# Toeplitz operands of 64 rows instead of 128, read from eight shifted copies of each head's taps

## The chip, the cores and the metric

One Trainium2 chip, one of its cores. The metric is the device time of one execution in microseconds (us), as a median over runs. Lower is better.

## What is computed

The input x is (64 batches, 32 heads, 512 positions), float32. The first layer is a causal convolution along the positions: each head has a filter of 512 taps, made from 64 complex modes, and the result is kept only where the position is below the batch's length. Added to x, it goes through a gated linear layer with low-rank (LoRA) additions chosen per batch. The case is about the first layer.

```python
def _get_kernel(log_dt, C, log_A_real, A_imag, length):     # K: the taps, heads x 512
    ...
    K = 2.0 * jnp.einsum('hn,hnl->hl', Cs, jnp.exp(P)).real
...
y = jnp.fft.irfft(u_f * k_f, n=n)[..., :Lq]                 # causal convolution of u with K
y = y + u_m * D[:, None]
return y * mask[:, None, :]
...
x = x + _L0_cond_ref(x, ...)        # convolution layer
x = x + _L1_cond_ref(x, ...)        # gate, up, silu, down, each with a low-rank part
```

## The kernel before

**Stages.** From 0 to about 20 us the taps of head group 0 are prepared; from there to about 79 us the convolution of 16 pairs of heads runs, with the taps of groups 1 to 3 prepared in between; from 80 us to the end the second layer runs, 16 tiles of 128 rows, with TensorE almost always busy.

**Taps.** The 32 heads are four groups `g` of eight. For each, VectorE makes phases (`phases(g)`), ScalarE sines (`trig(g)`), VectorE tables (`tables(g)`), TensorE multiplies them (`taps(g)` in the tensor block, L1025), and VectorE copies the result to `k_sb` (`taps(g)` in the vector block, L786 and L787), which raises `k_ready`. `store_taps(g)` writes the 16 KB to the DRAM tensor `kpad` (L255), a row for each head: 128 zeros and then 512 taps. A pair of heads is `pair`, so that group `g` holds the pairs 4g to 4g+3.

**Convolution.** A Toeplitz matrix is a window that slides over the taps: partition p of it is the row of taps shifted by p. `load_toep` (L261) builds it with one DMA from `kpad`: 128 partitions x 2 heads x 512 elements, each partition starting one element later, 512 KB for a pair. `load_um` (L266) loads the pair's input (256 KB), with its 128 positions of a block in reverse order. `conv(pair)` (L1038) makes eight float32 matmuls, four for each head: 128 rows are contracted, 128 columns of weights are `toep`, and 256, 192, 128 and 64 columns of `um` stream through. A float32 matmul appears in the trace as two weight loads and two matmuls, so a pair is 16 of each. Both heads' results share one PSUM bank of 512 columns. `add_conv(pair)` (L814) on VectorE selects the result into `x` with one COPY_PREDICATED of 128x512.

**Rings.** `toep`, `um` and the PSUM banks `ps_c` each have RC = 4 slots: `load_um` and `load_toep` wait on `conv_ps` until the pair four before is done, and `conv` waits on `x1_ok` until the pair four before has been added.

**Order.** All transfers are issued by SyncE (SP) in one written order, and a wait in it holds back everything behind it. After group 0 is stored come one weight piece (L244, 352 KB), the four `toep` of pairs 0 to 3, three more pieces, half of x for group 1 (512 KB), and so on; from pair 8 on a loop issues `um` and `toep` pair by pair, with the first LoRA tables among them (`a_raw`, four of 152 KB, behind pair 8; `b_raw`, four of 64 KB, behind pair 9), and behind it the six pieces of `wd`. On VectorE the order is `phases(1)`, `phases(2)`, `tables(1)`, `phases(3)`, `taps(1)`, the copy of `amask_t`, `add_conv(0)`, `tables(2)`, `tables(3)`, `taps(2)`, `add_conv(1)`, `taps(3)`, and then the pairs. On TensorE it is taps 0, pair 0, taps 1, pairs 1 and 2, taps 2, pair 3, taps 3, and then pairs 4 to 15. GpSimd makes the low parts of eight weight pieces (L439) once all taps are ready. ScalarE makes their high parts.

## Time and profile before

| | |
|---|---|
| median of 3 runs | 532.95 us (532.25 to 535.38) |
| the profiled execution: its time | 533.11 us |
| the profiled execution: span of the core | 531.4 us |
| the profiled execution: mean granted TensorE clock | 0.997 |
| TensorE matmul busy | 494.7 us (93%) |
| VectorE / ScalarE / GpSimd busy | 292.3 / 198.0 / 46.4 us |
| DMA traffic | 82.74 MB, mean 156 GB/s |

The span in 40 slices of 13.3 us each. A digit is the busy share of a slice in tenths, PEclk the granted clock in tenths of full speed, DMA the mean busy share of the 16 DMA engines. The convolution stage is in slices 3 to 6: there DMA stands at 9, and TensorE has slices below 9.

```profile
## 2 busy tenths in 40 slices
PE   0098799999999999999999999999999999999997
PEld 0087787989898999999999999898989898989986
DVE  7883176846454555546464547373737474545541
PEclk9999899999999999999999999999999999999999
DMA  7899995556555656555555656464646465555520
GB/s 288 267 346 376 331 340 128 122 111 154 116 152 115 144 128 147 126 137 118 142 123 138 130 129 139 108 157 109 157 88 174 101 161 114 153 117 148 110 63 21
```

A timeline row is start, duration, engine, line, operation, output<-input, shapes, count. PE is TensorE's matmul, PEld its weight load, SPq the queue of SyncE.

### The profile page before, as it was taken

The page shows a single profiled execution, that of the slowest core. Times are in us where ns is not written, and L with a number is a line of the kernel's source. Part 1 is how long each engine was busy: PE and PEld are TensorE (multiplying, and loading weights), DVE is VectorE, ACT ScalarE, POOL GpSimd, SP SyncE. Part 2 cuts the span into 40 slices and gives each one's busy share as a digit, 9 for nine tenths or more (in the row PEclk, how much of TensorE's full clock was granted, in tenths as well). Part 3 has the DMA queues.
Part 4 walks back from the last instruction along what each step waited for, and adds up shares of the span by engine and source line. Part 5 has one row for each costly group of instructions (what it writes and reads, how often), then busy time and mean ns, then how long its engine had stood idle before and what let it go on. Part 6 is the DMA issues. An engine that isn't in the chain of part 4 may idle for free.

```text
span 531.4 us, 9990 instructions
## 1 busy us (share of the span) xinstructions
PE 494.7 (93%) x2940; PEld 449.0 (84%) x2940; DVE 292.3 (55%) x617; ACT 198.0 (37%) x411; POOL 46.4 (9%) x55
## 2 busy tenths in 40 slices
PE   0098799999999999999999999999999999999997
PEld 0087787989898999999999999898989898989986
DVE  7883176846454555546464547373737474545541
ACT  5791006433333334334342333243434243434330
POOL 1006600100000001000000101010101010101000
PEclk9999899999999999999999999999999999999999
DMA  7899995556555656555555656464646465555520
GB/s 288 267 346 376 331 340 128 122 111 154 116 152 115 144 128 147 126 137 118 142 123 138 130 129 139 108 157 109 157 88 174 101 161 114 153 117 148 110 63 21
DMA packets 175443, 82.74 MB, mean 156 GB/s; under 512 B 128034, under 2 KB 157282, under 8 KB 175426
## 3 DMA queue, kind: packets, MB, share of 16 engines
q1 hardware_dynamic: 175426, 82.54, 60.5%
q8 instruction: 8, 0.13, 0.1%
q14 instruction: 9, 0.07, 0.0%
HBM read 63.46 MB, written 19.04 MB: 155 GB/s over the span
## 4 chain that ended last, share of the span: by engine, by line
PE 88%; DMA 5%; DVE 5%; issue 1%; SPq 0%; ACT 0%; DVEq 0%
PE ps_g L1111 23%; PE ps_u L1111 22%; PE ps_db L1072 13%; PE ps_da L1072 13%; PE ps_x L1064 3%; PE ps_g L1038 3%; DMA toep<-kpad 2%; DMA kpad<-k_sb 2%; PE ps_g L1121 2%; PE ps_u L1122 2%; PE ps_g L1122 2%; PE ps_u L1121 2%; PE ps_u L1038 2%; PE ps_da L1178 1%; PE ps_db L1179 1%
## 5 line engine op out<-in xcount | busy, mean ns | idle before, releaser
L1111 PE MATMUL ps_g<-w_hi,x_hi 128*128 128x512 f32 (+1 forms) x192 | 72.7, 379 | 1.4 <-DVE x_lo L995 1.4
L529 ACT CAST b_spl<-b_raw 64x512 fp32r<-64x512 f32 (+1 forms) x96 | 51.7, 571 | 55.3 <-PE ps_u L1122 35.7
L1111 PE MATMUL ps_u<-w_lo,x_hi 128*128 128x512 f32 (+1 forms) x192 | 71.4, 372 | 0.0
L1111 PE MATMUL ps_u<-w_hi,x_lo 128*128 128x512 f32 (+1 forms) x192 | 71.4, 372 | 0.0
L1111 PE MATMUL ps_g<-w_hi,x_lo 128*128 128x512 f32 (+1 forms) x192 | 71.4, 372 | 0.0
L1111 PE MATMUL ps_u<-w_hi,x_hi 128*128 128x512 f32 (+1 forms) x192 | 71.4, 372 | 0.0
L1111 PE MATMUL ps_g<-w_lo,x_hi 128*128 128x512 f32 (+1 forms) x192 | 70.9, 369 | 0.0
L876 DVE TENSOR_TENSOR b_spl<-b_raw,b_spl 64x512 fp32r<-64x512 f32 (+1 forms) x96 | 57.9, 629 | 15.3 <-ACT b_spl L529 13.7
L933 DVE TENSOR_TENSOR h_act<-h_act,ps_u 128x512 f32<-128x512 f32 (+1 forms) x48 | 30.4, 632 | 58.6 <-PE ps_u L1122 38.9
L1072 PE MATMUL ps_da<-wd_hi,ht_hi 128*128 128x288 f32 (+1 forms) x176 | 52.1, 296 | 0.0
L1072 PE MATMUL ps_da<-wd_lo,ht_hi 128*128 128x288 f32 (+1 forms) x176 | 51.9, 295 | 0.0
L1072 PE MATMUL ps_db<-wd_lo,ht_hi 128*128 128x288 f32 (+1 forms) x176 | 51.9, 295 | 0.0
L1072 PE MATMUL ps_db<-wd_hi,ht_hi 128*128 128x288 f32 (+1 forms) x176 | 51.9, 295 | 0.0
L1072 PE MATMUL ps_db<-wd_hi,ht_lo 128*128 128x288 f32 (+1 forms) x176 | 51.9, 295 | 0.0
L1072 PE MATMUL ps_da<-wd_hi,ht_lo 128*128 128x288 f32 (+1 forms) x176 | 51.8, 294 | 0.0
L464 POOL COPY xt<-x 128x512 f32 (+1 forms) x15 | 13.7, 911 | 397.1 <-DMA a_raw<-atab 397.1
L543 ACT CAST ht_hi<-h_raw 128x512 fp32r<-128x512 f32 (+1 forms) x45 | 24.7, 548 | 49.4 <-DMA h_raw<-hrow 49.4
L1111 PEld LDWEIGHTS ps_g<-w_hi,x_hi 128*128 128x128 f32 x192 | 36.1, 188 | 5.8 <-issue 1.5
L1111 PEld LDWEIGHTS ps_u<-w_hi,x_lo 128*128 128x128 f32 x192 | 36.1, 188 | 5.8
L1111 PEld LDWEIGHTS ps_u<-w_hi,x_hi 128*128 128x128 f32 x192 | 36.1, 188 | 5.8
L1111 PEld LDWEIGHTS ps_u<-w_lo,x_hi 128*128 128x128 f32 x192 | 36.1, 188 | 5.8
L1111 PEld LDWEIGHTS ps_g<-w_hi,x_lo 128*128 128x128 f32 x192 | 36.0, 188 | 5.7
(170 smaller groups left out, 887.7 us busy)
## 6 DMA issues: line engine op xcount, KB each, us to landing
a_raw<-atab SPq DMA_DIRECT2D x64, 152.0 KB, 2.3
toep<-kpad SPq DMA_DIRECT2D x16, 512.0 KB, 7.3
b_raw<-btab SPq DMA_DIRECT2D x128, 64.0 KB, 2.1
h_raw<-hrow SPq DMA_DIRECT2D x30, 256.0 KB, 2.9
um<-xr SPq DMA_DIRECT2D x16, 256.0 KB, 5.4
x<-xT SPq DMA_DIRECT2D x8, 512.0 KB, 6.9
w_raw<-wgu SPq DMA_DIRECT2D x8, 512.0 KB, 9.1
xrow<-x_sq SPq DMA_DIRECT2D x64, 64.0 KB, 2.2
```

The costliest lines, as they stand in the source:

```text
L464: nc.gpsimd.tensor_copy(xt[:, :, :].rearrange("p k (h b) -> p k h b", b=BT), x[:, :, :, bass.ds(t * BT, BT)].rearrange("p h k b -> p k h b ...
L529: nc.scalar.copy(b_spl[b_rows(slot), up, 0:w], b_raw[b_rows(slot), up * w:(up + 1) * w]).then_inc(b_hi, 1)
L543: nc.scalar.copy(ht_hi[:, f0:f0 + full, :], raw[:, 0:full, :]).then_inc(hthi_ok, 1)
L876: V.tensor_tensor(b_spl[b_rows(1 - slot), up, 0:w], b_raw[b_rows(slot), up * w:(up + 1) * w], b_spl[b_rows(slot), up, 0:w].bitcast(F32), A ...
L933: V.tensor_tensor(h_act[:, 0:w], h_act[:, 0:w], ps_u[s][:, 0:w], ALU.mult).then_inc(act_ok, 1)
L1038: last = T.matmul(ps_c[slot][:, at + d * NB:at + KB * NB], toep[:, slot, h, d * P:(d + 1) * P], v, start=(d == 0), stop=(d == KB - 1))
L1064: ins = T.matmul(ps_x[0][:, 0:P], w, xt[:, kb, :], start=(kb == 0), stop=(kb == KB - 1))
L1072: ins = T.matmul(ps[:, 0:c1 - c0], hs[0:rows, f, :], ws[0:rows, f, c0:c1], start=(f == 0 and hs is ht_hi and ws is wd_hi), stop=(bank == 1 ...
L1111: T.matmul(ps[:, 0:w], xs[:, kb, :], ws[:, kb, col:col + w], start=(kb == 0 and xs is x_hi and ws is w_hi), stop=False)
L1121: T.matmul(ps[:, 0:w], t_hi[:, up, :], b_spl[:, up, 0:w], start=False, stop=False)
L1122: T.matmul(ps[:, 0:w], t_lo[:, up, :], b_spl[:, up, 0:w], start=False, stop=True).then_inc(u_ps if up else g_ps, 1)
L1178: T.matmul(ps_da[:, 0:DA_W], ts[:, :], bd_spl[:, 0:DA_W], start=False, stop=end)
```

## The change

Both heads of a pair are handled side by side in 64 rows each. A Toeplitz operand for a head has now 64 partitions of HW = 576 elements; head 0 of the pair lies in partitions 0 to 63, head 1 in 64 to 127. A block of 128 positions is contracted in two halves of 64, so a head needs eight matmuls of 64 rows instead of four of 128. The matmuls alternate between the two heads, and each head writes a PSUM bank of its own (columns 0 to 255 of it). The rings become six slots for `toep` and `um` (RT, RU) and three double banks for the results (RP), one of them `ps_x`.

For group 0 each head's operand is loaded straight from `kpad`, two DMAs for a pair. For groups 1 to 3 a new DRAM tensor `krep` holds, for each head, eight copies of the taps, each shifted by eight elements (NCP = 8, ROWS = 8); `copy_taps(g)` writes them from `kpad` with one DRAM-to-DRAM DMA for the group, and `load_toep` reads both heads over 128 partitions with one DMA. The order of transfers is written anew, and on VectorE `taps(1)` moves ahead of `phases(3)`.

```diff
+RT = 6
+RU = 6
+RP = 3
+HR = P // 2
+HW = NL + HR
+NCP = 8
+ROWS = HR // NCP
+CW = HW + ROWS
...
+        krep = nc.dram_tensor("krep", (NH * NCP, CW), F32, kind="Internal")
...
-            toep = sb(pa, "toep", [P, RC, 2, NL])
-            um = sb(pa, "um", [P, RC, 2 * KB * NB])
+            toep = sb(pa, "toep", [P, RT, HW])
+            um = sb(pa, "um", [P, RU, 2 * KB * NB])
...
+        ps_c = [top.enter_context(nc.psum_tensor(name, [P, 2, 512], F32)) for name in ("ps_gg", "ps_uu", "ps_xx")]
+        ps_g, ps_u, ps_x = ([both[:, i, :] for i in range(2)] for both in ps_c)
...
-            return bass.AP(tensor=kpad, offset=pair * (2 * (P + NL)) + 1, ap=[[1, P], [P + NL, 2], [1, NL]])
+        def direct_taps(pair, h):
+
+            return bass.AP(tensor=kpad, offset=(2 * pair + h) * (P + NL) + 1, ap=[[1, HR], [1, HW]])
+
+        def copied_taps(pair):
+
+            return bass.AP(tensor=krep, offset=2 * pair * NCP * CW, ap=[[CW, 2 * NCP], [1, ROWS], [1, HW]])
...
+            def copy_taps(g):
+
+                sp.wait_ge(k_out[g], 16)
+                from_ = bass.AP(tensor=kpad, offset=g * HG * (P + NL) + 1, ap=[[P + NL, HG], [ROWS, NCP], [1, CW - 1]])
+                into = bass.AP(tensor=krep, offset=g * HG * NCP * CW, ap=[[NCP * CW, HG], [CW, NCP], [1, CW - 1]])
+                sp.dma_start(into, from_).then_inc(k_rep[g], 16)
+
+            def load_toep(pair):
+
+                slot, g = pair % RT, pair // RC
+                if g == 0:
+                    sp.wait_ge(k_out[0], 16)
+                    for h in range(2):
+                        sp.dma_start(toep[h * HR:(h + 1) * HR, slot, :], direct_taps(pair, h)).then_inc(toep_in[slot], 16)
+                else:
+                    sp.wait_ge(k_rep[g], 16)
+                    wait(sp, conv_ps, pair - RT + 1)
+                    sp.dma_start(toep[:, slot, :], copied_taps(pair)).then_inc(toep_in[slot], 16)
...
             store_taps(0)
+            for pair in range(RC):
+                load_toep(pair)
             load_piece(2 * KB)
-            for pair in range(RC):
-                load_toep(pair, pair, 0)
-            for n in range(2 * KB + 1, NP_GU):
-                load_piece(n)
+            load_piece(2 * KB + 1)
             load_x(1, 0)
+            for pair in range(RC, RU):
+                load_um(pair)
             store_taps(1)
             load_x(1, 1)
             load_x(2, 0)
...
+            copy_taps(1)
+            for pair in range(RU, 2 * RC - 1):
+                load_um(pair)
+            load_toep(RC)
+            load_um(2 * RC - 1)
+            load_toep(RC + 1)
+            load_toep(RC + 2)
+            load_x(2, 1)
+            store_taps(2)
+            load_toep(RC + 3)
+            load_um(2 * RC)
+            copy_taps(2)
+            store_taps(3)
+            load_x(3, 0)
+            copy_taps(3)
+            load_toep(2 * RC)
+            load_um(2 * RC + 1)
+            load_toep(2 * RC + 1)
+            load_piece(2 * KB + 2)
+            load_x(3, 1)
+            load_piece(2 * KB + 3)
...
+            taps(1)
             phases(3)
-            taps(1)
...
             def conv(pair):
-                slot = pair % RC
-                pe.wait_ge(toep_in[slot], 16 * (pair // RC) + 16)
-                pe.wait_ge(um_in[slot], 16 * (pair // RC) + 16)
-                wait(pe, x1_ok, pair - RC + 1)
-                for h in range(2):
-                    at = h * KB * NB
-                    for d in range(KB):
-                        v = um[:, slot, h * KB * NB:h * KB * NB + (KB - d) * NB]
-                        last = T.matmul(ps_c[slot][:, at + d * NB:at + KB * NB], toep[:, slot, h, d * P:(d + 1) * P],
-                                        v, start=(d == 0), stop=(d == KB - 1))
+                slot = pair % RT
+                pe.wait_ge(toep_in[slot], toep_need(pair))
+                pe.wait_ge(um_in[pair % RU], 16 * (pair // RU) + 16)
+                wait(pe, x1_ok, pair - RP + 1)
+                if pair == RP - 1:
+                    pe.wait_ge(amaskt_ok, 1)
+                for d in range(KB):
+                    for half in range(2):
+                        at = d * P + (1 - half) * HR
+                        for h in range(2):
+                            rows = slice(h * HR, (h + 1) * HR)
+                            v = um[rows, pair % RU, half * KB * NB:half * KB * NB + (KB - d) * NB]
+                            last = T.matmul(ps_c[pair % RP][:, h, d * NB:KB * NB], toep[rows, slot, at:at + P], v,
+                                            start=(d == 0 and half == 0), stop=(d == KB - 1 and half == 1))
                 last.then_inc(conv_ps, 1)
```

## Rows read from the trace of the kernel before

**Rows 1.** Chain of work that ended last, 15 to 82 us: start, us, what.
```profile
22.15 5.37 DMA toep<-kpad
27.56 4.95 PE ps_g L1038 x16
39.85 9.13 DMA kpad<-k_sb
...
79.03 0.20 DVE x L822
```

**Rows 2.** Timeline of TensorE: pairs 0 to 4, taps, and later pairs.
```profile
27.56 4.95 PE L1038 MATMUL ps_g<-um,toep 128*128 128x256 f32 x16 [7.55 <-DMA toep<-kpad]
32.44 0.96 PE L1025 MATMUL ps_db<-e 128*32 128x16 f32 x16
42.78 2.62 PE L1038 MATMUL ps_g<-um,toep 128*128 128x256 f32 x16 [0.66 <-DMA toep<-kpad]
46.82 2.62 PE L1038 MATMUL ps_g<-um,toep 128*128 128x256 f32 x16 [1.42 <-DMA toep<-kpad]
...
60.26 4.29 PE L1038 MATMUL ps_g<-um,toep 128*128 128x256 f32 x16 [2.08 <-DMA toep<-kpad]
64.39 4.98 PE L1038 MATMUL ps_u<-um,toep 128*128 128x256 f32 x32
69.20 4.98 PE L1038 MATMUL ps_g<-um,toep 128*128 128x256 f32 x32
74.01 4.98 PE L1038 MATMUL ps_u<-um,toep 128*128 128x256 f32 x32
```

**Rows 3.** Busy time by stretch: us, busy (x) by engine, PEclk, DMA share, GB/s.
```profile
42.78:64.38 21.60, 17.00 (x96) 15.57 (x97) 4.78 (x7) 1.14 (x2) 16.32 (x8) 0.92 1.06 371
62.00:64.00 2.00, 2.00 (x9) 1.82 (x9) 0.00 (x0) 0.42 (x1) 2.00 (x2) 0.53 1.10 398
```

**Rows 4.** DMA issues of 0 to 100 us: name, count, size, median us to landing.
```profile
toep<-kpad SPq DMA_DIRECT2D x16, 512.0 KB, 7.3
```

**Rows 5.** Landing times of `toep`, `um` and `kpad` (by tile), in this order.
```profile
DMA to landing us min/median/max: 4.1/7.3/10.0
...
DMA to landing us min/median/max: 2.8/5.4/9.3
...
DMA to landing us min/median/max: 1.5/7.2/10.0
```

**Rows 6.** Timeline of TensorE's weight loads at 70.12 us.
```profile
70.12 0.30 PEld L1038 LDWEIGHTS ps_g<-um,toep 128*128 128x128 f32 x2
```

**Rows 7.** Line 1038, 69 to 74 us: duration ns min/median/max of a weight load.
```profile
L1038 PEld LDWEIGHTS ps_g<-um,toep x32: 190/191/192, 69.1 to 73.8; 128*128 128x128 f32 x32
```

**Rows 8.** Timeline of VectorE between the first taps and the third.
```profile
29.37 0.55 DVE L723 TENSOR_TENSOR rr<-small,lvec 128x384 f32<-128x384 f32 x1
31.93 0.36 DVE L734 TENSOR_SCALAR ab<-rr 128x384 int32<-128x384 int32 x1
33.44 0.28 DVE L786 COPY k_sb<-ps_db 32x128 f32<-32x128 f32 x1 [1.15 <-PE ps_db L1025]
...
33.97 0.73 DVE L814 COPY_PREDICATED x<-lmask,ps_g 128x512 f32<-128x512 int32 x1
34.59 0.54 DVE L800 SCALAR_TENSOR_TENSOR gg<-th,gg 128x384 int32<-128x384 int32 x1
36.97 0.55 DVE L800 SCALAR_TENSOR_TENSOR gg<-th,gg 128x384 int32<-128x384 int32 x1
39.35 0.27 DVE L786 COPY k_sb<-ps_da 32x128 f32<-32x128 f32 x1
```

**Rows 9.** Timeline of SyncE's queue: first store of taps, first `toep`, and `wd`.
```profile
20.60 0.35 SPq L255 DMA_DIRECT2D kpad<-k_sb  x1
22.15 1.92 SPq L261 DMA_DIRECT2D toep<-kpad  x4
...
70.24 3.19 SPq L244 DMA_DIRECT2D wd_raw<-wd  x6
```

More of the change, by code:

```diff
@@ L143, in program @@
         ht_lo = sb(top, "ht_lo", [P, FB, P], F32R)
-        ps_g = [top.enter_context(nc.psum_tensor(f"ps_g{i}", [P, 512], F32)) for i in range(2)]
-        ps_u = [top.enter_context(nc.psum_tensor(f"ps_u{i}", [P, 512], F32)) for i in range(2)]
+        ps_c = [top.enter_context(nc.psum_tensor(name, [P, 2, 512], F32)) for name in ("ps_gg", "ps_uu", "ps_xx")]
+        ps_g, ps_u, ps_x = ([both[:, i, :] for i in range(2)] for both in ps_c)
         ps_da = top.enter_context(nc.psum_tensor("ps_da", [P, 512], F32))
         ps_db = top.enter_context(nc.psum_tensor("ps_db", [P, 512], F32))
-        ps_x = [top.enter_context(nc.psum_tensor(f"ps_x{i}", [P, 512], F32)) for i in range(2)]
         ps_k = [ps_da, ps_db]
-        ps_c = [ps_g[0], ps_g[1], ps_u[0], ps_u[1]]
         prm_in, len_in, idx_in = sem("prm_in"), sem("len_in"), sem("idx_in")
@@ L165, in program @@
         k_out = [sem(f"k_out{g}") for g in range(NG)]
-        toep_in = [sem(f"toep_in{i}") for i in range(RC)]
-        um_in = [sem(f"um_in{i}") for i in range(RC)]
+        k_rep = [sem(f"k_rep{g}") for g in range(NG)]
+        toep_in = [sem(f"toep_in{i}") for i in range(RT)]
+        um_in = [sem(f"um_in{i}") for i in range(RU)]
         conv_ps, x1_ok = sem("conv_ps"), sem("x1_ok")
@@ L255, in store_taps, with load_um @@
                 sp.dma_start(taps_rows(g), k_sb[:, g, :, :]).then_inc(k_out[g], 16)
-            def load_toep(pair, slot, group):
-                sp.wait_ge(k_out[group], 16)
-                wait(sp, conv_ps, pair - RC + 1)
-                sp.dma_start(toep[:, slot, :, :], shifted_taps(pair)).then_inc(toep_in[slot], 16)
-            def load_um(pair, slot, first):
-                if not first:
-                    sp.wait_ge(conv_ps, pair - RC + 1)
-                sp.dma_start(um[:, slot, :], xr[bass.ds(pair * P, P), :]).then_inc(um_in[slot], 16)
+            def copy_taps(g):
[13 more added lines that the diff above has]
+                    sp.dma_start(toep[:, slot, :], copied_taps(pair)).then_inc(toep_in[slot], 16)
+            def load_um(pair):
+                wait(sp, conv_ps, pair - RU + 1)
+                sp.dma_start(um[:, pair % RU, :], xr[pair * P:(pair + 1) * P, :]).then_inc(um_in[pair % RU], 16)
             def indices(a, q):
@@ L285, in _ @@
             for pair in range(RC):
-                load_um(pair, pair, True)
+                load_um(pair)
             load_x(0, 0)
@@ L303, in _ @@
             load_x(2, 0)
-            for pair in range(RC, 2 * RC):
-                load_um(pair, pair - RC, False)
-                load_toep(pair, pair - RC, 1)
-                if pair == RC:
-                    load_x(2, 1)
-                if pair >= RC + 2:
-                    store_taps(pair - RC)
-                    load_x(3, pair - RC - 2)
+            copy_taps(1)
+            for pair in range(RU, 2 * RC - 1):
+                load_um(pair)
+            load_toep(RC)
[16 more added lines that the diff above has]
+            load_piece(2 * KB + 3)
             def load_b(a, q, c, ids):
@@ L341, in store @@
                 sp.dma_start(out[bass.ds(t * P, P), :], y_sb[:, q, :]).then_inc(y_out, 16)
-            for pair in range(2 * RC, PAIRS):
-                load_um(pair, pair % RC, False)
-                load_toep(pair, pair % RC, pair // RC)
-                if pair == 2 * RC:
+            for pair in range(2 * RC + 2, PAIRS):
+                load_um(pair)
+                load_toep(pair)
+                if pair == 2 * RC + 2:
                     load_a(0, 0, ids0)
-                if pair == 2 * RC + 1:
+                if pair == 2 * RC + 3:
                     sp.wait_ge(mask_done, KB + 1)
```

11 lines of the change are left out of this document (7 added, 4 removed).

## Prediction

> **What bounds the kernel now.** I read the chain of waits first. From 22 to 79 us it passes through the convolution stage, by two kinds of link: TensorE in its pairs, and DMA, that is a `toep` load (5.37 us before pair 0) and a store of taps (9.13 us) [rows 1]. From 80 us on it is TensorE alone to the end, so whatever the change does to the moment when the last pair is done moves the end by the same amount; nothing behind that moment is touched. The timeline of TensorE then shows how far the stage is from its floor. The last pairs run back to back: two pairs start 4.81 us apart (64.39, 69.20, 74.01), 2.405 us a pair. Pair 4 starts at 42.78 and the last result is there at 79.03, so the twelve pairs 4 to 15 take 36.25 us where 12 x 2.405 = 28.9 would do [rows 1, 2]. The missing 7.4 us are waits on `toep` (pairs 4, 5 and 9 show 0.66, 1.42 and 2.08 us) and pair 9 itself, which took 4.29 us instead of 2.4 since it started at half clock behind a gap (0.53 of full in 62 to 64 us, which is the 1.2 GHz level) [rows 2, 3]. The busy table says who is late: from 42.78 to 64.38 the DMA engines are full (share 1.06) at 371 GB/s while TensorE works 17.0 of 21.6 us [rows 3]. So the stage is bound by DMA bytes up to 64 us and by TensorE after it. What can be won is about 7 us there, and some at the head of the stage.
>
> **Bytes.** Sixteen `toep` loads of 512 KB [rows 4] become 128 partitions x 576 x 4 B = 288 KB: 3.6 MB less. Three copies are added, 8 heads x 8 images x 583 x 4 B = 0.15 MB each. At 371 GB/s [rows 3] the saving is 3.1 / 0.371 = 8.5 us of transfer time, more than the 7.4 us that are missing. DMA can therefore stop being the bound; the rest of the sum is about what bounds instead.
>
> **Start of the stage.** Store of group 0 at 20.60, landed at 22.15 as before [rows 9]. A `toep` lands in 4.1 us at best for 512 KB, a `um` in 2.8 for 256 KB [rows 5]: about 1.5 us fixed and 2.6 for each 512 KB. For 288 KB that makes 3.0 us, plus one more issue of 0.48 us (four took 1.92 [rows 9]), and no weight piece runs ahead of it now; the next operands share the engines, so I take 3.65 where it was 5.37. Pair 0 starts at 25.8 instead of 27.56.
>
> **The taps of groups 1 to 3.** Pair 0 starts cold as before and takes 4.95 us, taps(1) about 0.9 [rows 2]: 31.7. VectorE copies them at once instead of at 33.44 (0.5 us) [rows 8], so group 1 is stored at 32.2, not 33.9. But VectorE now does `phases(3)` behind that, 2.9 us (29.37 to 32.29) [rows 8]; it idles meanwhile, and the work that filled its wait is late: `phases(3)` ends at 35.1, `amask_t` and `add_conv(0)` at 36.0, tables 2 and 3 take 2.4 each (34.59, 36.97, 39.35 [rows 8]), so the third taps are copied at 40.8 to 41.2 instead of 39.8. The new wait of pair 2 on `amask_t` (its bank is `ps_x`) holds TensorE until 35.3; pair 2 to 37.7, taps 2 after tables 2 at 38.4 to 39.1, pair 3 to 41.5, taps 3 to 42.2. The ring of three banks costs nothing: pair 4 wants `add_conv(1)`, done at 41.9, and later the additions (0.73 us each [rows 8]) keep well ahead. So pair 4 can start at 42.2, which is hardly earlier than 42.78: here the move on VectorE takes back what the faster start gave.
>
> **The copies, and the operands behind them.** A DRAM-to-DRAM copy is not in this trace. Below, it costs 1.5 us, the quickest landing out of `k_sb`; above, 9.13, the slowest store in the chain [rows 1, 5]. I take 3.5, near the 2.8 of a load with similar bytes, some more for its two ends in DRAM. Group 1: stored 32.2, landed 34.0, copied 37.5, pair 4's operand 3.0 to 4.1 later, at about 41.5: in time by 0.7 us. Group 2: stored at 41.2 behind about 0.8 MB still queued (1.6 MB issued from 37.5 on), landed 44.8, copied 48.3, operand of pair 8 at 51.5 to 52; wanted at 42.2 + 4 x 2.4 = 51.8. SP stands still in both waits; behind it in the queue stand `um`, x and the rest, and they lose some 7 us of issuing. Then the supply: from 48.3 on, up to pair 10, 2.6 MB at 371 GB/s are 7 us, plus landing 57.6, wanted 56.6; with the 0.6 MB of `a_raw` pair 11 comes at 60.5, wanted 59.0; pair 12 at 62.6, wanted 61.4; after that it gains on TensorE. Shortfall 1.5 us. The Trainium skill (DMA: Bandwidth & Descriptors, on why a DMA increments its semaphore by 16) says that a transfer runs on the largest number of engines up to 16 that divides its outer dimensions: eight for this copy, all sixteen for the load out of the images. No row here shows it. By it the copy would be at 0.4 us more (an estimate from 0.15 MB at 371 GB/s, doubled), which leaves the sum as it is.
>
> **The pair on TensorE: the open price.** A pair goes from 16 loads and matmuls of 128 rows to 32 of 64 rows with the same columns. If the two heads' matmuls run side by side, in different rows of the array, a pair stays at 2.4 us. If nothing overlaps it is 4.81, twice the 2.405 of [rows 2]. Between them lies the weight load: two loads of 128 columns take 0.30 us together, of which one lasts 0.19, so the second starts 0.11 us after the first [rows 6, 7]; beside matmuls of 64 columns that is the spacing. If loads follow one another while matmuls overlap, a pair costs 32 x 0.111 = 3.55 us. No 64-row pair is in the trace, so the bounds are 2.4 and 4.8; I take 2.4. The Trainium skill (TensorEngine Tiling (Array Packing), Key Properties) says that tiles of different rows can load weights and multiply in parallel: by it 2.4. The same skill (TensorE: Matmul & The Clock Gate, LDWEIGHTS) says that a load's time goes by its columns and not its rows: with loads one at a time, 3.55 us. The first is what I forecast, the second a rival below.
>
> **Sum.** 42.2 + 12 x 2.405 = 71.1, plus 1.5 of shortfall: 72.6 instead of 79.03, a gain of 6.4 us. Waiting less on operands, no pair starts at half clock. The six `wd` loads, issued at 70.24 now [rows 9], can go from about 60 on and meet nothing. Weight pieces 10 and 11 come later, about 55 us, and are wanted by VectorE at pairs 12 and 13 only. The profiled execution took 533.1 us (span 531.4); 533.1 - 6.4 = 526.7, and the median is 0.16 lower: 526.5.
>
> **Rivals.** (1) Loads one at a time, slower. For it: the load's 0.11 us spacing, the only thing of this kind that rows show [rows 6, 7]; against: nothing but that loads of other rows were never tried here. Pair 0 at half clock for 5.6 us and then fast, to 32.2; taps 1 32.9; pairs 1 and 2 to 40.0; taps 2, pair 3, taps 3 to 44.9; 12 x 3.55 = 42.6: 87.5, so +8.5, 541.5 us. It decides from a pair of about 2.8 us on: 6.4 us over 15 pairs are 0.43 each. (2) No overlap at all, a pair of 4.81: by the same chain pair 4 at 49.9 and the end at 107.6, +28.6, 561.5 us. (3) TensorE as forecast, but the supply stays the bound: each copy in a full queue costs up to 9.1 us instead of 3.5, or the reads slow down together. For it: SP's waits behind a store, 9.13 us [rows 1]; against: the queue is shorter by 3.1 MB. With half of the difference, 2.8 us, on each copy, group 1 is copied at 40.3; SP stands until then, so group 2 is stored at 42.4, landed 47.2, copied 53.5, and pair 8's operand is there at 56.8 instead of 51.8. With the same 1.5 us of shortfall behind it the end is 71.1 + 5.0 + 1.5 = 77.6, a gain of 1.4: 531.5 us, within 1% (527.6 to 538.3).
>
> **How the numbers follow.** Forecast 0.50, rival 1 0.22, rival 2 0.10, rival 3 0.18. The forecast's own range is 523.5 to 528.5: below, a supply without shortfall (1.5) and pairs shorter than 2.4, as the short matmuls would no longer wait on loads, down to the streams' share (1.5 more); above, a shortfall of 3.5. Rival 3 lies at 531.5. The range is carried up over rival 1 to 543 and leaves out rival 2. A measurement here can tell about 1% from no change. Faster by over 1% is gain above 5.3 us: 0.48, nearly all of the forecast. Within 1%: 0.21, rival 3 and what lies between 2.6 and 3.3 us a pair. Slower: 0.31, rivals 1 and 2.
>
> **What would show it.** TensorE's timeline: late pairs 2.4 us apart (right), 3.5 (rival 1) or 4.8 (rival 2). Busy table: DMA share well below 1 in parts of 42 to 65 us, TensorE near full. Waits: `toep` under 3 us after pair 4; more, and after an idle queue, is rival 3. Third taps copied near 41 us. First matmul of the second layer near 74 instead of 80.37. The prediction falls if the pair's spacing is not 2.4 us, or if a copy takes over 6 us.

## The result, and the profile after

The changed kernel takes 542.05 us (538.96 to 542.5) beside 533.54 us (532.25 to 535.38) for the kernel before: a ratio of 1.0144, 95% interval 1.0095 to 1.0194. It is slower by about 1.4%, which is clear of the noise, where 526.5 us were forecast. The profiled execution took 542.5 us with a span of 540.7 (before 533.1 and 531.4).

The timeline of TensorE of the changed kernel, lines of `conv` (L1085) and the first lines of the second layer; columns as in [rows 2]:

```profile
26.05 4.96 PE L1085 MATMUL ps_gg<-um,toep 64*128 64x256 f32 x32 [6.16 <-DMA toep<-kpad]
...
43.08 2.62 PE L1085 MATMUL ps_uu<-um,toep 64*128 64x256 f32 x32 [1.08 <-DMA toep<-krep]
45.53 2.57 PE L1085 MATMUL ps_xx<-um,toep 64*128 64x256 f32 x32
47.94 2.57 PE L1085 MATMUL ps_gg<-um,toep 64*128 64x256 f32 x32
50.39 2.62 PE L1085 MATMUL ps_uu<-um,toep 64*128 64x256 f32 x32
58.33 4.28 PE L1085 MATMUL ps_xx<-um,toep 64*128 64x256 f32 x32 [5.32 <-DMA toep<-krep]
62.45 2.57 PE L1085 MATMUL ps_gg<-um,toep 64*128 64x256 f32 x32
67.86 4.28 PE L1085 MATMUL ps_uu<-um,toep 64*128 64x256 f32 x32 [2.84 <-DMA toep<-krep]
73.26 2.62 PE L1085 MATMUL ps_xx<-um,toep 64*128 64x256 f32 x32 [1.12 <-DMA toep<-krep]
76.57 2.62 PE L1085 MATMUL ps_gg<-um,toep 64*128 64x256 f32 x32 [0.69 <-DMA toep<-krep]
79.03 2.57 PE L1085 MATMUL ps_uu<-um,toep 64*128 64x256 f32 x32
81.43 2.57 PE L1085 MATMUL ps_xx<-um,toep 64*128 64x256 f32 x32
83.84 2.57 PE L1085 MATMUL ps_gg<-um,toep 64*128 64x256 f32 x32
88.20 0.47 PE L1158 MATMUL ps_gg<-w_hi,x_hi 128*128 128x512 f32 x1 [1.79 <-DVE x_lo L1038]
...
89.34 0.63 PE L1158 MATMUL ps_gg<-w_lo,x_hi 128*128 128x512 f32 x1
```

Three things are to be read here. First, pairs that are not kept waiting start 2.41 us apart (43.08, 45.53, 47.94, 50.39, and 79.03, 81.43, 83.84), just as before the change [rows 2]: the 32 short matmuls of a pair cost what the 16 long ones did. Second, pair 8 (58.33) waits 5.32 us, pair 10 2.84, pair 11 1.12 and pair 12 0.69, all on `toep`; pairs 8 and 10, behind the longer gaps, start at half clock (PEclk 0.50 in 57 to 61 us and 0.57 in 68 to 72) and take 4.28. By itself that costs nothing here, since the next operands were later still: pair 10's landed at 67.8, pair 11's at 73.2, pair 12's at 76.5, and from there the pairs run back to back. Third, the last result is there at about 86.4 (83.84 plus a pair) and not at 79.03, and the second layer starts at 88.20 instead of 80.37, 7.8 us later. Another 1.5 us goes there: seven of its first matmuls last 0.63 us and start 0.43 apart, where in the kernel before they last 0.40 and start 0.23 apart. The granted clock is 0.50 in 90 to 92 us; TensorE had stood still for 1.79 us before them. In the kernel before it stood still for 1.38 us at this place and the clock stayed at 1.00. 7.8 and 1.5 are the 9.3 us by which the span is longer.

The chain of work that ended last shows where pair 8's operand was:

```profile
32.18 4.31 DMA kpad<-k_sb
36.50 3.16 DMA krep<-kpad
...
42.17 0.59 SPq L267
42.76 0.04 issue
42.80 6.95 DMA kpad<-k_sb
49.77 0.69 SPq L279
50.47 0.04 issue
50.51 3.01 DMA kpad<-k_sb
53.53 0.68 SPq L279
54.22 0.05 issue
54.29 0.03 issue
54.32 0.56 SPq L291
...
62.29 10.93 DMA toep<-krep
73.22 0.04 issue
73.26 2.65 PE ps_xx L1085 x32
```

Group 2's store of 16 KB took 6.95 us to land. SyncE stood in `copy_taps(2)` for it, issued that copy, stored group 3 and stood again until that store had landed (3.01 us), since `copy_taps(3)` is written ahead of `load_toep(8)`. The first operand of group 2 was issued at 54.32. Its copy had been issued at 49.77 and had landed at 53.04, so of the second stand only 1.3 us were lost: the rest ran beside the copy.

The busy table (columns as in [rows 3]) shows what SyncE's standing did, and then that the transfers behind it were slow:

```profile
48.00:52.00 4.00, 4.00 (x50) 3.80 (x50) 1.47 (x2) 0.00 (x0) 3.89 (x2) 1.00 0.42 115
52.00:56.00 4.00, 1.02 (x20) 0.88 (x16) 0.72 (x1) 0.00 (x0) 0.00 (x0) 0.86 0.63 168
...
68.00:72.00 4.00, 4.00 (x32) 3.81 (x32) 0.00 (x0) 0.00 (x0) 1.36 (x2) 0.57 1.08 208
72.00:76.00 4.00, 2.76 (x34) 2.40 (x32) 2.19 (x3) 1.14 (x2) 4.00 (x2) 1.00 1.05 232
76.00:80.00 4.00, 3.43 (x42) 3.25 (x44) 4.00 (x3) 0.00 (x0) 4.00 (x3) 1.00 1.06 243
```

In 48 to 52 us the DMA engines are busy to 0.42 and move 115 GB/s, where the kernel before moved about 400. From 68 us on they are full (1.05 to 1.08) and move only 208 to 243 GB/s, where [rows 3] has 371 at the same busy share. The table of DMA issues gives the loads by their size:

```profile
toep<-krep SPq DMA_DIRECT2D x12, 288.0 KB, 8.1
```

288 KB take 8.1 us to land (median), where 512 KB took 7.3 [rows 4].

So there are two losses. Forecast were pair 8 at 51.8 and the end at 72.6. **Loss A**: pair 8 starts at 58.33, 6.5 us late. **Loss B**: back to back from there it would have ended at 58.33 + 8 x 2.405 = 77.6, and it ended at 86.4, 8.8 us later, of which 1.5 were forecast. 6.5 and 7.3 are the 13.8 us between 72.6 and 86.4. (The half clock of pairs 8 and 10 lies within loss B and adds nothing to it, as said above.) The experiments take the two apart.

### The profile page after: what moved, and what is told of

Its sections match the earlier page's. It is cut to its first block, busy times and chain, and to the rows that moved or that the text cites. A ratio compares the mean times of both kernels' runs of the same rounds, so it can differ in the third digit from the quotient of the medians.

```text
span 540.7 us, 10507 instructions
## 1 busy us (share of the span) xinstructions
PE 497.9 (92%) x3196; PEld 452.0 (84%) x3196; DVE 297.2 (55%) x617; ACT 198.1 (37%) x411; POOL 47.4 (9%) x55
## 4 chain that ended last, share of the span: by engine, by line
PE 84%; DMA 7%; DVE 5%; SPq 2%; issue 1%; ACT 0%; DVEq 0%
PE ps_gg L1158 23%; PE ps_uu L1158 22%; PE ps_db L1119 13%; PE ps_da L1119 13%; DMA kpad<-k_sb 3%; PE ps_xx L1111 3%; DMA toep<-krep 2%; PE ps_gg L1168 2%; PE ps_uu L1169 2%; PE ps_gg L1169 2%; PE ps_uu L1168 2%; DVE w_lo L872 1%; PE ps_gg L1085 1%; PE ps_da L1225 1%; SPq L291 1%
## 5 line engine op out<-in xcount | busy, mean ns | idle before, releaser
L1158 PE MATMUL ps_gg<-w_hi,x_hi 128*128 128x512 f32 (+1 forms) x192 | 73.3, 382 | 1.8 <-DVE x_lo L1038 1.8
L1158 PE MATMUL ps_gg<-w_hi,x_lo 128*128 128x512 f32 (+1 forms) x192 | 71.9, 375 | 0.0
L1158 PE MATMUL ps_gg<-w_lo,x_hi 128*128 128x512 f32 (+1 forms) x192 | 71.6, 373 | 0.0
L1158 PE MATMUL ps_uu<-w_hi,x_lo 128*128 128x512 f32 (+1 forms) x192 | 71.4, 372 | 0.0
L1158 PE MATMUL ps_uu<-w_lo,x_hi 128*128 128x512 f32 (+1 forms) x192 | 71.4, 372 | 0.0
L1158 PE MATMUL ps_uu<-w_hi,x_hi 128*128 128x512 f32 (+1 forms) x192 | 71.4, 372 | 0.0
L572 ACT CAST b_spl<-b_raw 64x512 fp32r<-64x512 f32 (+1 forms) x96 | 51.8, 571 | 44.2 <-PE ps_uu L1169 35.7
L1119 PE MATMUL ps_da<-wd_hi,ht_lo 128*128 128x288 f32 (+1 forms) x176 | 51.8, 294 | 0.0
L1158 PEld LDWEIGHTS ps_gg<-w_hi,x_hi 128*128 128x128 f32 x192 | 36.4, 190 | 6.3 <-issue 1.9
L1158 PEld LDWEIGHTS ps_gg<-w_hi,x_lo 128*128 128x128 f32 x192 | 36.5, 190 | 5.8
L1158 PEld LDWEIGHTS ps_uu<-w_hi,x_lo 128*128 128x128 f32 x192 | 36.1, 188 | 5.8
L1158 PEld LDWEIGHTS ps_uu<-w_hi,x_hi 128*128 128x128 f32 x192 | 36.1, 188 | 5.8
```

The lines of the kernel that those rows point to most:

```text
L572: nc.scalar.copy(b_spl[b_rows(slot), up, 0:w], b_raw[b_rows(slot), up * w:(up + 1) * w]).then_inc(b_hi, 1)
L1119: ins = T.matmul(ps[:, 0:c1 - c0], hs[0:rows, f, :], ws[0:rows, f, c0:c1], start=(f == 0 and hs is ht_hi and ws is wd_hi), stop=(bank == 1 ...
L1158: T.matmul(ps[:, 0:w], xs[:, kb, :], ws[:, kb, col:col + w], start=(kb == 0 and xs is x_hi and ws is w_hi), stop=False)
```

## Experiments

All start from the changed kernel, but the one that says it starts from the kernel before. "The rate" is that of the busy table, in stretches of 4 us; the kernel before has 272, 337 and 399 GB/s at 68, 72 and 76 us. Where a run is said to be a single execution, its time is a single one; the rates are always those of one execution.

### The two losses, one at a time

**Without the copies** (loss A):

```diff
-                    sp.wait_ge(k_rep[g], 16)
-                    wait(sp, conv_ps, pair - RT + 1)
-                    sp.dma_start(toep[:, slot, :], copied_taps(pair)).then_inc(toep_in[slot], 16)
+                sp.wait_ge(k_out[g], 16)
+                wait(sp, conv_ps, pair - RT + 1)
+                for h in range(2):
+                    sp.dma_start(toep[h * HR:(h + 1) * HR, slot, :], direct_taps(pair, h)).then_inc(toep_in[slot], 16)
...
-            copy_taps(1)
...
-            copy_taps(2)
...
-            copy_taps(3)
```

> The changed kernel without the DRAM copies: groups 1 to 3 are loaded like group 0, two loads of 64 partitions for a pair, straight from the rows of taps, and SyncE waits for the store only. Everything else is as changed. Theory A (the chain store, copy, load with SyncE standing in it is what is lost): pair 8 starts about 3 to 4 us earlier than 58.3, near 54, and the end is 4 to 8 us earlier than in the changed kernel, 534 to 538 us. Theory B (loads of Toeplitz rows slow all transfers down to some 235 GB/s, whatever they are read from): the rate from 64 to 80 us stays near 235 GB/s, and the end is within 3 us of 542. Theory C (the images are what slows the transfers): both vanish, the stage ends near 73 us and the time is 527 to 530 us.

Measured: 535.02 us (532.13 to 536.62), ratio to before 1.0034, interval 1.0006 to 1.0062; span 534.4. By the ratios, 1.1 of the 1.44% are back, some 6 us. Pairs 4 to 9 run back to back, and pair 8 starts at 54.94 instead of 58.33 without a wait, but the transfers stay slow: pairs 10 and 11 wait 2.30 and 1.97 us and the rate is 251 and 262 GB/s at 68 and 72 us. Each direct load is two issues (1.09 us of SyncE a pair instead of 0.54), and that did not outweigh what the copies and their waits cost.

**With the copies and their waits, but loads from rows apart** (loss B): the twelve loads of groups 1 to 3 read 128 separate rows of another tensor, 2304 bytes each, in one stride.

```diff
-                    sp.dma_start(toep[:, slot, :], copied_taps(pair)).then_inc(toep_in[slot], 16)
+                    apart = bass.AP(tensor=xr.tensor, offset=(pair - RC) * P * HW, ap=[[HW, P], [1, HW]])
+                    sp.dma_start(toep[:, slot, :], apart).then_inc(toep_in[slot], 16)
```

> The changed kernel, but the Toeplitz loads of pairs 4 to 15 read 128 rows of 2304 bytes that lie one behind the other in the input instead of overlapping rows of the images, so the values of those pairs are wrong; the copies, the waits, the sizes and the order are kept. Theory B or C (overlapping rows in DRAM are read slowly): the packets of 2304 bytes take 93 to 100 ns instead of 137 on average, the rate from 68 to 82 us rises from 235 to about 390 GB/s, pairs 9 to 15 follow one another at 2.4 us, and the stage ends 6 to 8 us earlier than 86.4. Theory A (only the waits of SyncE count): the rate stays at 235 and the end is within 1 us of the changed kernel's 540.7 span.

Measured, a single execution: 535.58 us, span 533.8. Here the rate is restored:

```profile
68.00:72.00 4.00, 3.76 (x46) 3.58 (x48) 2.79 (x3) 1.14 (x2) 4.00 (x3) 1.00 1.05 386
72.00:76.00 4.00, 4.00 (x59) 3.87 (x56) 3.24 (x4) 0.00 (x0) 4.00 (x2) 1.00 1.05 387
```

386 and 387 GB/s for the same bytes in rows of the same length. So the chain of store, copy and load is one loss, and something in how the loads read or are described is another.

**Both**: rows apart, and no copies and no waits for them.

> Both suspected losses taken away together: no DRAM copies and no wait for them (as in the direct kernel), and the Toeplitz loads of pairs 4 to 15 read 128 rows that lie apart in the input (values of those pairs wrong), one load for a pair. If the two causes, the chain store, copy, load and the slow overlapping reads, are all that kept the forecast from coming true, the pairs 4 to 15 run nearly back to back, the stage ends at 72 to 74 us and the time is 526 to 528 us. If another loss is left (the weight pieces and the tables in between, the clock), it is 530 us or more.

Measured: 528.7 us (527.37 to 530.2), ratio 0.9913, interval 0.9884 to 0.9943; span 528.5. The spans nearly add up: 540.7 without either, 534.4 with the first alone (-6.3), 533.8 with the second alone (-6.9), 528.5 with both (-12.2). Since the first run has no copies and this one has none either, one load in one stride instead of two half loads is worth 5.9 us (534.4 to 528.5); since the second and this one read the same rows, the copies and their waits alone are worth 5.3 (533.8 to 528.5). The time lies between the two ranges of the expectation: a third loss is left. Pairs 4 to 9 run back to back from 40.72, and the last starts at 73.58 and ends near 76.0. That is 3.4 us behind the forecast 72.6, although pair 4 starts 1.5 us earlier than forecast; back to back from 40.72 the stage would end at 69.6, so the shortfall is 6.4 us where 1.5 were forecast. It goes through pairs 10 and 11 (1.75 and 2.50 us of waiting, and pair 11 at half clock). They wait for loads that ran in this stretch, where four `b_raw` loads of 64 KB run among them:

```profile
57.00:61.00 4.00, 2.62 (x32) 2.39 (x32) 1.20 (x2) 0.00 (x0) 1.20 (x2) 1.00 1.06 239
```

Behind it, at 64 and 68 us, the rate is 389 and 386. The kernel before has 275 GB/s in 57 to 61, with its own four `b_raw` loads issued at 53.11. That the `b_raw` loads are what lowers the rate there is read from their packets (264 ns for 4096 bytes); no run took them away from beside fast loads. This kernel isn't one to use: the operands of pairs 4 to 15 come from the wrong tensor.

### Whether the move on VectorE matters

```diff
-            taps(1)
             phases(3)
+            taps(1)
```

> The changed kernel with one move undone: on VectorE phases(3) stands ahead of taps(1) again. Theory A (group 2's store, copy and load set when pair 8 starts): the third taps are copied about 1 us earlier than 40.4, pair 8 starts about 1 us earlier, and the time falls by about 1 us, to 541. Theory B (the rate of the transfers sets the end): no change beyond 0.5 us.

> The direct loads (no copies) together with phases(3) ahead of taps(1) again. If the third taps' store sets the moment of pair 8 to 10 in the direct kernel, the end comes 0.5 to 1 us earlier than with direct loads alone (535.0), about 534; if the rate of the loads does, it is the same within 0.5 us.

The first is the changed kernel with only this edit: 541.58 us, ratio 1.0158 (1.0122 to 1.0193). Group 1 is stored at 32.78 instead of 32.18, group 2 at 43.55 instead of 42.80, pair 8 starts at 59.26. The second has the edit beside the direct loads: 534.57 us, ratio 1.0029 (1.0009 to 1.0048), against 1.0034 without it. Neither shows a difference in time: where `phases(3)` stands is neither the loss nor a cure. Pair 8 was expected earlier with the old order, if the store of group 2 set its start, and came 0.9 us later, since that store too was issued later.

### What makes the loads slow

The load out of the images differs from a load of rows apart in several ways at once: its rows overlap, they start at addresses one element apart, and its source is described as sixteen groups of eight rows, as [[CW, 16], [1, 8], [1, HW]]. Each run changes one of them; each is a single execution. The DMA engine that moved a row is not in these traces: which rows go to which engine, on which the expectations of the sliding and the same rows and of the larger direct loads build, no run shows. In each the copies and the waits stay, unless said otherwise.

**Alignment.** Rows apart, 577 elements apart instead of 576, starting one element on.

> As the kernel whose rows lie apart (pairs 4 to 15 from the input, values of those pairs wrong), but the rows are 577 elements apart and start one element in, so that they do not overlap and nearly all start off a 64-byte boundary. Theory M (misaligned starts are what makes the loads slow): the rate in 68 to 76 us is back near 235 to 250 GB/s, the packets of 2304 bytes take 150 ns and more. Theory O (overlap is: many reads of the same few KB of DRAM): the rate stays near 390 GB/s and the packets at 93 to 105 ns.

Measured: 538.02 us; 386, 389 and 343 GB/s at 68, 72 and 76 us. The start of a row doesn't slow it. (Its time is 2.4 us above the other run with rows apart, which is on another chip and a single execution too; I don't read that difference.)

**Length.** Rows of 2048 bytes out of the images instead of 2304.

> The changed kernel with Toeplitz rows of 2048 bytes instead of 2304 for pairs 4 to 15, read from the same images with the same shifts; matmuls that need the last 64 columns take the columns before them, so the values are wrong. Theory L (the odd row length of 2304 bytes is what is slow): packets of 2048 bytes take 84 to 90 ns as in the kernel before and the rate in 68 to 78 us is near 390 GB/s. Theories M and O: the rate stays near 235 GB/s, the stage ends about 1 us earlier only, for the bytes.

Measured: 540.66 us; 202, 268 and 274 GB/s. Slow: it isn't the length.

**The same rows again and again, and sliding rows.** Sixteen rows that start whole, each read eight times ([[HW, 16], [0, 8]]); groups that slide by one whole row ([[HW, 16], [HW, 8]]); and the same eight rows for all sixteen groups ([[0, 16], [HW, 8]]).

> As the kernel whose rows lie apart, but 16 rows of 2304 bytes, each at a 64-byte boundary, are read eight times each instead of 128 rows once (values of pairs 4 to 15 wrong). Full overlap without misalignment. Theory O: near 235 GB/s in 68 to 78 us. Theory M: near 390 GB/s and a stage end as with the rows apart, 80.2 us.

> Overlap of another kind, values of pairs 4 to 15 wrong: DMA engine e reads the eight aligned rows e to e+7, so that each row is read up to eight times as before, but never twice running by the same engine and not by two engines at the same step. Theory R (what is slow is an engine's reading of the same few KB several times running): near 390 GB/s in 68 to 78 us. Theory S (many reads of a small region of DRAM by anyone, 37 KB or 53 KB): near 240 GB/s.

> All sixteen DMA engines read the same eight aligned rows (18 KB), one behind the other; values of pairs 4 to 15 wrong. Theory R: near 390 GB/s, since no engine reads a row twice running. Theory S: slower than with eight reads of each of 16 rows, 150 to 230 GB/s, since the region is half as large.

Measured: 540.32, 538.45 and 540.89 us; at 72 us 243, 226 and 262 GB/s. All slow, whatever the overlap between neighbours or between groups. What they have in common with the changed kernel is the description, 16 by 8, and that some bytes are read more than once. The next three separate these.

**Description against overlap.** First, 16 groups of 8 rows that don't overlap at all (groups nine rows apart, [[9 * HW, 16], [HW, 8], [1, HW]]). Second, one stride over 128 partitions with full overlap, one head's sliding window straight out of `kpad` ([[1, 128], [1, HW]]). Third, rows apart without overlap, as two loads of 64 partitions each.

> Rows that lie apart, as in the fast variant, but described like the load out of the images: sixteen groups of eight rows instead of 128 rows at one stride (values of pairs 4 to 15 wrong). Theory D (what is slow is how the description deals the partitions to the DMA engines): near 240 GB/s in 68 to 76 us, stage end 84 to 86 us. Theory S (overlapping reads of a small region of DRAM): near 388 GB/s, stage end near 80 us.

> One window of 128 rows at a stride of one element over one head's taps, 2304 bytes each, one load for a pair (values of pairs 4 to 15 wrong): fully overlapping, but described like the load of the kernel before. Theory D: near 388 GB/s in 68 to 76 us. Theory S: near 240 GB/s.

> Rows that lie apart, loaded in two loads of 64 partitions for a pair, as the direct kernel does (values of pairs 4 to 15 wrong); copies and waits as changed. Theory D in the form that half the partitions is what slows the direct kernel: near 255 GB/s. Theory S: near 388 GB/s and a stage end near 80 us.

Measured: 540.42, 536.82 and 542.61 us. The stretch at 72 us, sixteen groups of eight without overlap:

```profile
72.00:76.00 4.00, 3.63 (x23) 3.32 (x25) 1.26 (x1) 1.14 (x2) 4.00 (x3) 0.57 1.06 263
```

one stride over 128 partitions, full overlap:

```profile
72.00:76.00 4.00, 4.00 (x46) 3.72 (x46) 3.88 (x3) 0.00 (x0) 4.00 (x3) 0.89 1.06 388
```

two loads of 64 partitions, no overlap:

```profile
72.00:76.00 4.00, 3.15 (x24) 2.79 (x23) 2.16 (x2) 0.02 (x1) 3.64 (x3) 0.50 1.06 236
```

The four corners are filled: one stride over 128 partitions is fast with overlap (388) and without (387), sixteen groups of eight are slow with it (232) and without (263). The last three and the run with rows apart differ from one another in their source rows, their description and, for the two halves, the number of loads only. My own theory up to then, that reads of the same bytes get in each other's way, is refuted in both directions. What decides is how the load is described and laid out over its partitions.

**Fewer, larger direct loads.** Direct loads, each one the 64-row half of two pairs.

> Direct loads from the rows of taps, no copies, values right; each load covers one 64-row half of two pairs, so that an engine's successive packets alternate between two heads, as in the kernel before. Theory R: the packets speed up to near 100 ns, the rate in 68 to 76 us rises above 300 GB/s, and the time is 529 to 532 us, faster than the direct kernel's 535.0. Theory S: the rate stays near 250 GB/s and the time is 534 to 536 us.

Measured: 536.98 us, ratio 1.0065 (1.0036 to 1.0095); 221 and 225 GB/s at 68 and 72 us. Half the issues, the same slow rate: two heads in one load don't mend a load onto 64 partitions. 529 to 532 us were expected had it mattered which rows an engine reads one after another.

**The `b_raw` loads.** Direct loads with the old order on VectorE, and the four `b_raw` loads moved behind the last pair's operand.

> Direct loads, phases(3) first, and the four b_raw loads of the first tile (4 KB rows onto 16 partitions each) moved behind the Toeplitz load of the last pair. All values right. In every trace so far the rate falls to about 200 to 240 GB/s for 3 us when packets of 4096 bytes of these loads run (300 ns each). If that stretch is what delays pairs 10 and 11, their waits fall from 3.7 us to under 1 us and the time falls by 2 to 4 us, to 531 to 533 us, level with the kernel before. If the overlapping loads are the cause, less than 1 us is gained.

Measured: 534.51 us, ratio 1.0034 (1.0007 to 1.0061), against 1.0029 with them in place. No gain, where 2 to 4 us were expected if they delayed pairs 10 and 11: beside loads that are slow anyway they aren't what binds. Whether moving them would pay with fast loads wasn't tried.

### Does it hold with the right values?

**The kernel before, with the other description of the same addresses.**

```diff
-ap=[[1, P], [P + NL, 2], [1, NL]]
+ap=[[8, P // 8], [1, 8], [P + NL, 2], [1, NL]]
```

> The kernel before with one edit: the Toeplitz load of a pair reads the same addresses into the same places, but its source is described as sixteen groups of eight rows instead of one stride over 128 partitions. Theory (the description alone sets the rate): the load of 512 KB in 2048-byte rows then runs at 200 to 270 GB/s in the stage instead of the 337 and 399 GB/s that the kernel before has at 72 to 80 us, the first convolution stage ends 3 to 8 us later, and the whole is slower, 536.5 to 541 us. Rival (it is something in the changed kernel around the loads, such as 2304-byte rows with fewer loads in flight): the time stays at 533 to 534 us with the stage's rates unchanged.

Measured: 533.81 us, ratio 1.0022 (0.9997 to 1.0047), and 293, 328 and 393 GB/s. By its expectation this speaks for the rival. But one thing in the trace makes it no test: sixteen groups that follow one another in one stride are the same as one stride over 128, and an issue of this load costs 0.39 us (median) as before (0.39), where no load of sixteen groups in these runs costs less than 0.53. The description was most likely joined again before it reached the queue; that isn't shown. I count the run as inconclusive.

**More images of fewer rows.** NCP = 16 instead of 8: sixteen images of four rows for each head, so that the load is 32 groups of four rows, and, in a second run, NCP = 64: one stride over 128 rows.

```diff
-NCP = 8
+NCP = 16
```

> The changed kernel with sixteen shifted images of four rows for each head instead of eight of eight: the load's source is 32 groups of four rows, the copy per group writes 295 KB + instead of 148 KB. Theory (what counts is how the outer dimension deals the rows; sixteen is the number at which all rows of one group go one way, and 32 may deal as sixteen does): if 32 groups run like sixteen, the rate in the stage stays at 200 to 250 GB/s and the time at 540 to 543 us; if it is the length of a run of neighbouring partitions that counts, the rate rises part of the way and the time falls to 536 to 539 us. Rival (the copy's size sets the wait at pair 8): pair 8 starts 1 us or more later than 58.3 us and the time is 543 us or more.

> The changed kernel with 64 images of one row each for each head, so that the load's source is one stride over 128 partitions, every row apart; the copy per group grows to 1.18 MB written and as much read. Theory (description sets the rate): the loads run at 350 GB/s or more where the copies don't run beside them, as in the runs with rows apart, while each copy takes 5 to 10 us in place of about 4, so pairs 4 and 8 start later than in the changed kernel; net 537 to 545 us. Rival (rows that came from a fresh DRAM copy load slowly, whatever the description): the rate stays at 200 to 250 GB/s and the time is 545 us or more.

With 16 images, measured 539.8 us (537.6 to 542.48), ratio 1.0134 (1.0084 to 1.0183). It computes the whole layer as the changed kernel does; the load has the same bytes in rows of the same length and overlaps as before, and the rate is restored:

```profile
72.00:76.00 4.00, 4.00 (x56) 3.85 (x54) 2.59 (x3) 1.14 (x2) 4.00 (x3) 1.00 1.06 391
76.00:80.00 4.00, 4.00 (x57) 3.82 (x55) 3.30 (x4) 0.00 (x0) 4.00 (x2) 1.00 1.05 387
```

391 and 387 against 232 and 243. Pairs 12 to 15 run back to back, and the second layer starts at 86.04 instead of 88.20. (The last pair is done 2.7 us earlier; half a microsecond of that goes to VectorE, for whose `x_lo` TensorE then waits 2.31 us instead of 1.79.) The expectation that 32 groups would be as slow as sixteen was wrong. Only 2.2 us come of it in the profiled execution (span 538.5 against 540.7), and the two ratios, 1.0134 and 1.0144, lie within each other's intervals. So the rate is shown to come back with right values, and a gain in time is not. The copies are twice as large and loss A stays: pair 4 starts at 43.59 at half clock behind 2.57 us of waiting, pair 8 at 59.40.

With 64 images, 555.62 us, ratio 1.0435 (1.0401 to 1.0469). Copies of 1152 KB take the queue: pair 8 waits 14.4 us. It is worse, in the range that its rival gave, though for the size of the copies and not for slow loads: once pair 8 has started, at 75.73, only one more pair waits, pair 11 for 1.13 us, where the changed kernel waits at pairs 10, 11 and 12. The rate was expected at 350 GB/s or more; it is 311 in 80 to 88 us and 363 in 85 to 95, with `toep` packets of 110 and 107 ns on average.

No version with right values was found that beats the kernel before. The best is the one with direct loads and the old order on VectorE, 0.3% slower (1.0029, interval 1.0009 to 1.0048). Not tried was 16 images with the store and the copy of group 3 written behind the first operands of group 2, which would leave the rate and shorten SyncE's second stand.

## Why the forecast was wrong, point by point

**The bound of before: right.** DMA and the waits on `toep`. **Bytes: right in count, wrong as an argument.** 288 KB instead of 512 were moved, as said, but "at 371 GB/s the saving is 8.5 us" took the rate over from a load of another form. This is the term that failed most in **the sum**: "2.6 MB at 371 GB/s are 7 us", shortfall 1.5. Measured were 208 to 243 GB/s in the stretch behind, and a shortfall of 8.8. The experiments showed that the rate goes with the layout of the load over its partitions: with rows in one stride it was 386 to 389 again. And a smaller part stayed even then: with one stride and no copies at all the shortfall was 6.4 us, with 239 GB/s in the stretch where `b_raw` runs. The sum took one rate for the whole way from 48.3 us on.

**Start of the stage: right.** Pair 0 started at 26.05, forecast 25.8. (The eight half loads of group 0 held SyncE for 5.00 us, 0.6 each, against 1.92 for four before [rows 9]; the forecast counted one of them more.) **VectorE: right.** Third taps were copied at 40.40 (forecast 40.8), `amask_t` held pair 2 to 35.26 (forecast 35.3), and pair 4 started at 43.08 (forecast 42.2).

**The copy itself: right, what stands around it: wrong.** The three copies took 3.2, 3.3 and 3.8 us from issue to landing (forecast 3.5). But the stores that feed the copies were taken at 1.8 and 3.6 us and landed in 4.31 and 6.95. And the walk from group 2 to pair 8 left out a step that stands in the diff: `store_taps(3)` and `copy_taps(3)` lie between `copy_taps(2)` and `load_toep(8)`, and a copy waits for its store in SyncE's own queue. Forecast were 41.2 stored, 44.8 landed, operand by 51.8; measured 42.80, 49.77 and 58.33. The 6.5 us of loss A are then: 1.6 because SyncE, back from its wait for the first copy at 39.66, had five issues of 0.6 us ahead of the store; 3.3 for the store's landing; 1.3 between the copy's landing (53.04) and the operand's issue (54.32), which is what the second stand and its issue cost; and the rest, 0.3, for the copy (3.3 instead of 3.5) and the operand's own landing (4.0 instead of 3.5). No run takes these apart; they are read from the one trace. The forecast named what is queued behind a wait, `um`, x and the rest, and not the next store and copy.

**The clock: wrong.** "No pair starts at half clock" was forecast; pairs 8 and 10 did (4.28 us each). It cost nothing there, but the same thing cost 1.5 us at the head of the second layer, and so "nothing behind that moment is touched" didn't hold either.

**The pair on TensorE: right.** It was called the open price, and 0.32 of the chances went to it. It costs 2.41 us, with weight loads of 64 rows lasting 188 ns, as those of 128 did (191) [rows 7]. Thirty-two loads in 2.41 us are one every 0.075 us. In this row ten of them take 0.95 us, and (0.95 - 0.19) / 9 = 0.085 us lie between their starts, where [rows 6] had 0.11, which is the price that the rival put on each:

```profile
81.38 0.95 PEld L1085 LDWEIGHTS ps_xx<-um,toep 64*128 64x128 f32 x10
```

A load every 0.075 us, lasting 0.188 each: 2.5 are under way at once on average, where 128-row loads were 1.3 (16 of 0.191 in 2.41 us). So the loads of 64 rows overlap more than the rival allowed; that it is those of the two heads that run side by side is how I read it. That 542.05 us lies near the 541.5 of this rival, and inside the range, is a coincidence of size: its mechanism didn't occur.

**What happened was rival 3, at three times its size.** It said that the supply stays the bound, by "each copy in a full queue" or because "the reads slow down together". The reads did slow down together. The full queue came true too, though for the stores and not for the copies, which took 3.2 to 3.8 us. The rival was priced with the queue alone, and with half of the difference at that: pair 8 at 56.8 (measured 58.33), no slower rate behind it, 531.5 us. (Its chain lets the store of group 2 take 4.8 us where the forecast has 3.6, without a reason; measured 6.95.) With the store at 9.13 us, which stood in [rows 1] for this very transfer, and with SyncE's second stand, the forecast's own chain puts pair 8 at about 58.4 and the end at 79.1, level with the kernel before; the slower transfers are what makes it slower. And the forecast held that `wd` "meets nothing" from 60 us on; it was issued at 70.54 and its six issues took 9.23 us, against 3.19 [rows 9].

## What to carry over

A price per byte belongs to a transfer's layout and not to its queue: when a change cuts bytes by changing the layout of a load, carry over the old rate only as the upper bound, and look first at whether the new one still lays 128 partitions in one stride. A new DRAM round trip costs not its copy alone (3.2 to 3.8 us here) but also the landing of the small store ahead of it in a loaded queue (4.3 to 7 us) and what the issuing queue holds back meanwhile; so walk the written order line by line past every wait. And where two losses lie behind one another, try both fixes together too: either alone gave 6 to 7 us here and left the kernel no faster than before, and only the run with both came out faster, by 0.9%, about two thirds of the forecast gain.

## What the runs showed of the hardware

**The rate goes with the layout.** At a DMA busy share of 1.04 to 1.08 throughout, at 72 to 76 us:

| load of 128 partitions x 2304 bytes | GB/s |
|---|---|
| one stride over 128 partitions, rows apart | 387 (386 in 68 to 72) |
| one stride over 128 partitions, rows overlapping | 388 (375 in 68 to 72) |
| 32 groups of four rows, overlapping | 391 |
| 16 groups of eight rows, overlapping / apart | 232 / 263 |
| two loads of 64 partitions, apart | 236 |

In the first two rows few of the packets at 72 to 76 us are those of `toep` (74 of 789 and 64 of 794); at 68 to 72 nearly half are (348 and 350), and the rate is the one in brackets.

It isn't these loads' own packets alone that grow slow. From the trace's packet records, 72 to 76 us, mean duration by size:

```
2048-byte packets (other loads):    before 100 ns   changed 147   rows apart, one stride 88   16 images 87
2304-byte packets (toep):                           changed 163   rows apart, one stride 99   16 images 99
```

The packets of 2048 bytes are those of other loads, `um` and `wd` above all (in the kernel before, `toep` too), and their form is the same in all four. They take 147 ns beside slow loads and 87 to 88 beside fast ones. So one badly laid out load costs the transfers beside it as well. In the changed kernel from 68 to 72 us, where `b_raw` runs too (64 KB onto 16 partitions, packets of 4096 bytes at 335 ns), the rate falls to 208.

The reason isn't shown by any run.
**Overlapping or unaligned rows did no harm.** 128 rows that each start one element on ran at 388 GB/s, rows of 577 elements' stride at 389.

**Issues have a price by form.** An issue of a load in one stride takes SyncE 0.38 us, of one in sixteen or 32 groups 0.53 or 0.54, of a load of 64 partitions 0.54 to 0.60, of a copy from DRAM to DRAM 0.7 to 0.8.

**A float32 pair in 64-row tiles costs the same.** Two heads in different rows of the array, 32 matmuls of 64 rows instead of 16 of 128, take the same 2.41 us, weight loads included.
